# Graph messages on one core: the transposes of the next tile, in a block or singly among the products

## What is computed

```
h    = relu(layernorm(x))                       # per row, eps 1e-5
m    = relu([h[src], h[dst]] @ W.T + b)         # one message of 512 per edge
out  = x + segment_sum(m, src)                  # messages added to the row of their source
```

## Time and profile before

| | |
|---|---|
| median of 3 runs | 874.6 us (872.36 to 884.21) |
| span of the profiled execution | 865.8 us |
| its own time | not given by the profile; the median is 8.8 us above the span |
| TensorE busy | 739.9 us, 85% of the span, 3430 matmuls |
| VectorE busy | 571.6 us, 66% |
| ScalarE busy | 481.1 us, 56% |
| GpSimd busy | 363.2 us, 42% |
| mean granted TensorE clock | 0.957 of full speed |
| moved by DMA | 188.92 MB in packets |

### The profile page before, as it was taken

The page is one execution under the profiler, slowest core; times in us unless marked ns, Lnnn a source line. Parts: engine busy times, 40 slices in busy tenths (PEclk is TensorE's granted clock), DMA queues, the critical chain, the costliest instruction groups (busy, mean ns, idle before and its releaser), DMA issues.

```text
span 865.8 us, 13768 instructions
## 1 busy us (share of the span) xinstructions
PE 739.9 (85%) x3430; PEld 594.0 (69%) x3430; DVE 571.6 (66%) x1874; ACT 481.1 (56%) x892; POOL 363.2 (42%) x304
## 2 busy tenths in 40 slices
PE   1897998998998999877999999887686969695993
PEld 1786876776886777656888888675575747574782
DVE  4776857858786576746787876647465647455761
ACT  3765656666675565544767676446364546444651
POOL 5322212222222221211226665656565665656732
PEclk9999999999999999998999999999988989897998
DMA  6999999999999999993225677768677766767753
GB/s 219 381 338 347 336 359 349 366 339 340 348 356 356 337 367 343 346 351 123 77 87 115 112 143 115 128 115 141 105 146 122 123 118 117 140 101 141 148 85 48
DMA packets 42411, 188.92 MB, mean 218 GB/s; under 512 B 7894, under 2 KB 14166, under 8 KB 40384
## 3 DMA queue, kind: packets, MB, share of 16 engines
q0 software_dynamic: 29792, 77.00, 42.6%
q1 hardware_dynamic: 5552, 105.39, 32.4%
q10 hardware_dynamic: 7056, 6.43, 3.4%
HBM read 163.19 MB, written 128.61 MB: 337 GB/s over the span
## 4 chain that ended last, share of the span: by engine, by line
DMA 47%; PE 29%; issue 12%; DVE 4%; POOL 3%; ACT 3%; POOLq 1%; ACTq 0%; DVEq 0%; SPq 0%
DMA xg<-x,dst_i 25%; DMA out<-ring,add_i 20%; PE z_ps L499 7%; PE z_ps L501 7%; PE z_ps L500 7%; PE ht_ps L483 4%; POOL out L197 2%; DMA src_row<-src_rows 2%; ACT h L395 1%; POOL xg L181 1%; DVE stats L232 1%; DVE zb L273 1%; PE agg_ps L511 1%; ACT ht_hi L386 1%; PE agg_ps L512 1%
## 5 line engine op out<-in xcount | busy, mean ns | idle before, releaser
L499 PE MATMUL z_ps<-w_hi,ht_hi 128*128 128x512 f32 x784 | 324.9, 414 | 2.4 <-DVE ht_lo L265 2.4
L500 PE MATMUL z_ps<-w_lo,ht_hi 128*128 128x512 f32 x784 | 314.6, 401 | 0.0
L501 PE MATMUL z_ps<-w_hi,ht_lo 128*128 128x512 f32 x784 | 314.3, 401 | 0.0
L181 POOL DMA_INDIRECT xg<-x,src_i x98 | 102.2, 1043 | 329.8 <-ACT h L395 295.4
L232 DVE BATCH_NORM_STATS2 stats<-xg 128x6 f32<-128x512 f32 x196 | 125.9, 684 | 169.2 <-DMA xg<-x,dst_i 165.9
L197 POOL DMA_INDIRECT out<-ring,add_i x98 | 158.3, 1615 | 135.4 <-DMA out<-ring,add_i 96.6
L386 ACT CAST ht_hi<-ht_ps 128x512 fp32r<-128x512 f32 x196 | 107.7, 589 | 187.1 <-PE ht_ps L483 185.0
L483 PE MATMUL ht_ps<-identity,h 128*128 128x128 f32 x784 | 115.6, 293 | 84.5 <-ACT h L402 84.5
L499 PEld LDWEIGHTS z_ps<-w_hi,ht_hi 128*128 128x128 f32 x784 | 151.9, 194 | 35.2 <-DVE ht_lo L265 2.8
L501 PEld LDWEIGHTS z_ps<-w_hi,ht_lo 128*128 128x128 f32 x784 | 150.1, 191 | 37.1
L500 PEld LDWEIGHTS z_ps<-w_lo,ht_hi 128*128 128x128 f32 x784 | 151.5, 193 | 32.4
(11 more groups left out here) (40 smaller groups left out, 396.2 us busy)
## 6 DMA issues: line engine op xcount, KB each, us to landing
out<-x SPq DMA_DIRECT2D x125, 800.0 KB, 8.7
src_row<-src_rows ACTq DMA_DIRECT2D x49, 128.0 KB, 5.1
ring<-w_t SPq DMA_DIRECT2D x4, 512.0 KB, 6.3
xg<-x,src_i POOLq DMA_INDIRECT x98, 5.3
xg<-x,dst_i POOLq DMA_INDIRECT x98, 6.4
out<-ring,add_i POOLq DMA_INDIRECT x98, 5.0
out<-x SPq DMA_DIRECT2D x1, 512.0 KB, 14.0
bias_bc<-bias SPq DMA_DIRECT2D x1, 256.0 KB, 13.0
```

The source lines that it names most:

```text
L181: nc.gpsimd.indirect_dma_start(out=xg[:, b, s, :], out_offset=None, in_=x, in_offset=bass.IndirectOffsetOnAxis(ap=nodes[:, t:t + 1], axis= ...
L499: nc.tensor.matmul(z_ps[b][:, :], hi, w_hi[:, c, :], start=(c == 0), stop=False)
L500: nc.tensor.matmul(z_ps[b][:, :], hi, w_lo[:, c, :], start=False, stop=False)
L501: last = nc.tensor.matmul(z_ps[b][:, :], lo, w_hi[:, c, :], start=False, stop=(c == K - 1))
```

## The change

The eight transposes of tile t+1 are no longer issued as a block before the products of tile t. They are issued singly among them: behind the products number 0, 2, 4, ..., 14 of the 24, so that one transpose stands between the first and second, the third and fourth, and so on, and 9 products follow the last one. The waits are those of before, now ahead of chunk 0 of each side, that is behind products 0 and 8. The semaphore `transposed` is raised by chunk 3 of each side, that is behind products 6 and 14. The number of instructions is the same. Tiles 0 and 1 keep their blocks. No other engine's code is touched.

```
-            def transposes(t, b):
-                for s in range(SIDES):
+            def transpose_chunk(t, b, s, k):
+                if k == 0:
                     pe.wait_ge(h_ready, SIDES * t + s + 1)
                     if not (isinstance(t, int) and t < 2):
                         pe.wait_ge(lo_ready, SIDES * (t - 2) + s + 1)
+                chunk = nc.tensor.transpose(ht_ps[b][s][:, k * P:(k + 1) * P],
+                                            h[:, b, s, k * P:(k + 1) * P], identity[:, :])
+                if k == KD - 1:
+                    chunk.then_inc(transposed, 1)
+
+            def transposes(t, b):
+                for s in range(SIDES):
                     for k in range(KD):
-                        last = nc.tensor.transpose(ht_ps[b][s][:, k * P:(k + 1) * P],
-                                                   h[:, b, s, k * P:(k + 1) * P], identity[:, :])
-                    last.then_inc(transposed, 1)
-
-            def products(t, b):
+                        transpose_chunk(t, b, s, k)
+
+            def products(t, b, beside=False):
...
-                        nc.tensor.matmul(z_ps[b][:, :], hi, w_hi[:, c, :], start=(c == 0), stop=False)
-                        nc.tensor.matmul(z_ps[b][:, :], hi, w_lo[:, c, :], start=False, stop=False)
-                        last = nc.tensor.matmul(z_ps[b][:, :], lo, w_hi[:, c, :], start=False, stop=(c == K - 1))
+                        terms = ((hi, w_hi), (hi, w_lo), (lo, w_hi))
+                        for n, (left, right) in enumerate(terms):
+                            m = 3 * c + n
+                            last = nc.tensor.matmul(z_ps[b][:, :], left, right[:, c, :], start=(m == 0),
+                                                    stop=(m == 3 * K - 1))
+                            if beside and m % 2 == 0 and m < 2 * K:
+                                transpose_chunk(t + 1, 1 - b, m // 2 // KD, m // 2 % KD)
                 last.then_inc(mm_done, 1)
...
-                if has(1):
-                    transposes(s + 1, 1 - b)
                 if has(0):
-                    products(s, b)
+                    products(s, b, has(1))
                 if not b and has(-2):
                     sums(s - 2)
```

## The result

The changed kernel takes 1026.4 us in the median against 878.4 for the kernel before in the same runs; the ratio is 1.169, with a 95% interval of 1.161 to 1.177. The forecast was 984 us, slower by 109; measured is slower by 148. The profiled execution took 1029.1 us with a span of 1027.4. In the later sessions, in which the experiments ran, the kernel before took 868 to 920 us; ratios compare the faster executions of each kernel, medians are of all.

The account below looks back on a forecast made before the run. The prediction took the chain of steps through each tile's late last transpose to bound the changed kernel: span 936.8 + 4.2 + 5.8 + 14.9 = 961.7, plus 8.8 gives 970.5, plus 13 for the clock gives 984 us; range 950 to 1030.

Parts of the forecast that it names:

- the ring through the last transpose: Loop of transposes, ScalarE's deviation, centring and division, next transposes: 3.3 us longer, with 1.9 us to spare on average.
- the dearer rivals: Two slower cases: much of the run at low clock (1049 us, chance 0.12), costly transpose/product turns (about 1045, chance 0.06).
- Slots of 0.233 and 0.109 us: TensorE's time per product and per transpose, claimed unchanged, with 0 us for the eight new turns between them.
- Dear turns: Rival: each transpose/product turn on TensorE costs 0.08 us, 0.6 us per interval; about 1045 us, chance 0.06.
- Odd step D + 8.64: Steps with ring copies: next last transpose 8.64 us after D, this step's last transpose start; the division decides.
- Even step D + 10.37: Steps with sums: next last transpose 10.37 us after D, this one's start; sums wait for m_lo, TensorE idles.
- The chain sets the whole run: Claim that the steps, 19.0 us a pair, set the pace throughout, not gathers or scatter-adds; span 961.7 us.
- The clock term: TensorE's low clock after even-step pauses: a third of 47 at 1.5 us, 24 us, about half counted: +13 us.
- The signs: Expected profile: TensorE about 78% busy, some 100 us waiting for m_lo, 36 and 12 to 13 tiles, first add 535 to 550.
- Low clock for much of the run: Rival: mixing transposes and products or pauses holds TensorE at 1.2 GHz for a quarter of the run; 1049 us, chance 0.12.
- Only one kind of step binds: Rival: the m_lo wait is met earlier, so even steps take 8.6 us too; 903 us, chance 0.07.
- not slower: Rival: the ring's slack hides the shift and transpose loads vanish under products, saving 7 us; 867 us, chance 0.04.

Follow-up runs that it names:

- early spread: Changed kernel with the eight transposes singly behind the first eight products instead of every second of sixteen: 906.9 us, ratio 1.012 to the kernel before.
- late block: Changed kernel with the eight transposes in one block behind the fifteenth product: 966.2 us, ratio 1.091 to the kernel before.
- Message first: Changed kernel with the message's high part (ScalarE) and low part (VectorE) moved ahead of tile s+1's high and low parts: 899.3 us, ratio 1.015 to before.
- filled pause: Changed kernel with nine unneeded products on TensorE before its wait for m_lo: 977.0 us, ratio 1.103 to the kernel before.
- copies last: Changed kernel with ScalarE's two ring copies of odd steps moved behind the division: 958.9 us, ratio 1.083 to the kernel before.
- six more: Changed kernel with six unneeded products behind the wait for m_lo, the pause left as it is: 1117.3 us, ratio 1.280 to the kernel before.

## Why the prediction was right and where it fell short

The direction and the mechanism held: the ring through the last transpose sets the pace, and the pause that it makes is priced by the clock. The range (950 to 1030) held with some luck. 1026 is 4 us inside its end and outside the forecast's own 955 to 1010; the room above 1010 was made for the dearer rivals, not for the term that needed it. By the steps of the prediction:

- Slots of 0.233 and 0.109 us and no price for the turns: right. The mixed stretch runs at 0.575 us per two products and a transpose. "Dear turns" is out, also by early spread and late block.
- Odd step D + 8.64, through copies and division: measured 8.55, and 7.71 when the copies are moved away.
- Even step D + 10.37, through m_lo: the single full-clock interval is 10.30, and 10.25 with the pause filled. Message first removes the wait and 2.5 us of the interval at full clock (7.83 against 10.30).
- "The chain sets the whole run": right. The span is 37.01 (last transpose of tile 2) + 48 x 8.53 + 47 x 11.83 + 24.95 = 1027.4. The last term was forecast as 24.9, the first as 34.66; the first transpose of tile 2 starts 0.8 us later in this execution (31.41), and a low stretch follows it.
- The clock term failed. "A third of them ... so I take +13": 46 of 47 pauses were followed by a low stretch, all on the chain, 46 x 1.57 = 72 us. The price of one was right (1.5 expected), the share was three times too small, and halving it for work off the chain was wrong, since behind this pause come the sums and the spread stretch, which both lie on it. I took the share from nine scattered pauses of the kernel before, where none returned in every round. This one term is more than the whole gap: 72 - 13 = 59 us more for the clock, 9 less from the intervals at full clock, 2 more at the start, 7 less for what lies around the span (1.7 us in this execution, not the 8.8 that I took from a median and another execution's span) and 3 less from the profiled execution to the median make 984 + 42, the 1026 measured.
- The signs: TensorE's share is 79% (78 forecast), the wait for m_lo 106.2 us over 48 (100 over 47), the windows have 34 and 12 tiles (36 and 12 to 13). GpSimd's first add comes at 573.1 us, later than the 535 to 550 forecast: 26 even intervals lie ahead of it, each with its low stretch.
- "Low clock for much of the run": in part right, 0.916 in the mean, which is 17% of the run at 1.2 GHz where the rival had 25%, and its 1049 us is nearer to 1026 than 984 is. But it came with the pause and not for the mixture alone, as filled pause shows. That a transpose does not count as activity of TensorE (the Trainium skill, "TensorE: Matmul & The Clock Gate", "Part 4: PE-mode transpose") is not refuted, since products surround them in each run here; as the only cause of this loss it is, because the transposes are as many in filled pause at a clock of 1.00.
- "Only one kind of step binds" and "not slower" are out by both intervals.
- The chances: the text gives the last rival 0.04 and then splits it into 0.02 and 0.03; the 0.95 for slower should be 0.96. Nothing hangs on it.

No version tried beats the kernel before.

## What to carry to other kernels

Where engines hand work round a ring, what counts is when the last piece of a batch is done, not how evenly its pieces are laid among other work; measure the ring's slack before spreading a producer (here 0.93 us were free in the middle stage, 3.3 were not). Spreading cost 1 to 2% instead of 17 when it was done early, or when other work that doesn't need the batch no longer stood behind it in the ordered lists of the engines that wait for it. And a short pause on TensorE that returns in every round has to be priced with the clock: by the share of rounds that a run shows, not by a few scattered pauses of another kernel.

## What was not expected of the hardware

A pause of 2.2 us was followed by a stretch at 1.2 GHz in 46 of 47 rounds here (TensorE's only other pauses in a round are 1.0 and 0.6 us), and in other shares in kernels with the same pause and a different length of round: 24 of 47 at 18.0 us a pair (copies last), 26 at 18.1 (late block), 46 at 18.9 (the change), 36 at 20.2 plus 24 behind shorter pauses (six more), each pair length being that without low stretches. In the changed kernel the low stretches return every 20.4 us, once a pair. The Trainium skill, "TensorE: Matmul & The Clock Gate", section "Why this matters for your kernels", warns only of longer pauses than these; these runs disagree. What decides between the rounds stays open; the rhythm proposed in six more was not it.
